# Scores of a key tile's two query halves in neighbouring PSUM banks, read by one exponential of 1024 columns

## The reference

```python
q = ln @ Wq
kv_input = jnp.concatenate((xn, ln), axis=1)
kv = kv_input @ Wkv
k, v = jnp.split(kv, 2, axis=-1)
...
q, k, v = (heads(q) * scale, heads(k), heads(v))
sim = jnp.einsum('bhid,bhjd->bhij', q, k)
mask_full = jnp.concatenate((mask, jnp.ones((b, m), dtype=bool)), axis=1)
...
sim = jnp.where(mask_full[:, None, None, :], sim, max_neg)
attn = jax.nn.softmax(sim.astype(jnp.float32), axis=-1).astype(sim.dtype)
out = jnp.einsum('bhij,bhjd->bhid', attn, v)
```

## Time and profile before

| | |
|---|---|
| time, 3 runs | median 810.05 us (809.28 to 811.12) |
| the profiled execution | 812.56 us, its span 810.8 us |
| granted TensorE clock, mean | 0.978 of full speed |
| PE busy | 751.5 us (93% of the span), 7122 matmuls |
| ACT busy | 609.7 us (75%), 1086 instructions |
| POOL busy | 545.3 us (67%), 745 |
| DVE busy | 559.9 us (69%), 1399 |
| HBM | 34 GB/s over the span |

### The profile page before, as it was taken

How to read it: one execution, slowest core, us unless ns; L and a number is a source line. 1 busy time by engine, 2 the same in 40 slices (tenths; PEclk the granted TensorE clock), 3 DMA queues, 4 the chain that set the end, 5 groups by cost and what they waited for, 6 DMA issues and landing times.

```text
span 810.8 us, 22755 instructions
## 1 busy us (share of the span) xinstructions
PE 751.5 (93%) x7122; PEld 418.6 (52%) x7122; DVE 559.9 (69%) x1399; ACT 609.7 (75%) x1086; POOL 545.3 (67%) x745
## 2 busy tenths in 40 slices
PE   5598999999999999999999999999999999899766
PEld 3344544556464555545554655555555546455423
DVE  5776776666666767666666667676766666586677
ACT  5479788887868687888878696868788887865262
POOL 4366676686867768686868677686868686766122
PEclk9799999999999999999999999999999999999797
DMA  5303322121222202121212212121212121110001
GB/s 178 79 6 93 78 75 73 43 61 56 57 60 56 58 17 63 45 71 42 63 52 58 58 55 62 32 58 32 71 45 72 40 60 56 47 43 19 4 1 53
DMA packets 95820, 44.42 MB, mean 55 GB/s; under 512 B 66500, under 2 KB 87848, under 8 KB 95656
## 3 DMA queue, kind: packets, MB, share of 16 engines
q1 hardware_dynamic: 95728, 43.93, 19.5%
q10 hardware_dynamic: 56, 0.05, 0.0%
HBM read 24.20 MB, written 3.34 MB: 34 GB/s over the span
## 4 chain that ended last, share of the span: by engine, by line
PE 65%; DVE 14%; issue 10%; ACT 5%; POOL 3%; DMA 1%; DVEq 1%; ACTq 0%; SPq 0%; POOLq 0%
PE bank L1496 14%; PE bank L1576 7%; PE bank L1459 6%; PE bank L1463 5%; PE bank L1461 5%; PE bank L1414 4%; PE bank L1593 3%; DVE mx L1940 3%; PE bank L1431 3%; PE bank L1611 2%; PE bank L1390 2%; DVE qkl_l L1936 2%; PE bank L1430 2%; PE bank L1648 1%; ACT qkl_h L1118 1%
## 5 line engine op out<-in xcount | busy, mean ns | idle before, releaser
L867 POOL TENSOR_TENSOR p<-arena,p 128x512 f16<-128x512 f32 x256 | 297.9, 1169 | 133.0 <-ACT arena L1137 131.9
L1146 ACT ACTIVATE p<-bank,maskbias 128x512 f16<-128x512 f32 x224 | 155.2, 693 | 103.5 <-PE bank L1463 101.5
L1496 PE MATMUL bank<-p,xv 128*128 128x512 f16 (+1 forms) x768 | 182.3, 380 | 5.3 <-POOL arena L915 3.7
L1940 DVE TENSOR_REDUCE mx<-bank 128x1 f32<-128x464 f32 x256 | 154.0, 632 | 17.8 <-PE bank L1431 16.1
L1137 ACT ACTIVATE arena<-bank,maskbias 128x512 f32<-128x512 f32 x224 | 155.0, 692 | 0.0
L1496 PEld LDWEIGHTS bank<-p,xv 128*128 128x128 f16 (+1 forms) x768 | 58.2, 97 | 74.5 <-issue 25.6
L1936 DVE TENSOR_TENSOR qkl_l<-bank,qkl_h 128x512 f16<-128x512 f32 x64 | 41.1, 686 | 68.9 <-ACT qkl_h L1118 68.8
L1459 PE MATMUL bank<-qkc_h,xtT_h 128*128 128x512 f16 (+1 forms) x256 | 86.5, 389 | 0.0
L1463 PE MATMUL bank<-qkc_h,xtT_l 128*128 128x512 f16 (+1 forms) x256 | 85.0, 379 | 0.0
L1461 PE MATMUL bank<-qkc_l,xtT_h 128*128 128x512 f16 (+1 forms) x256 | 85.0, 379 | 0.0
L1431 PE MATMUL bank<-xtT_h,qkc_h 128*128 128x400 f16 x256 | 83.4, 338 | 0.0
(11 more groups left out here) (283 smaller groups left out, 1576.0 us busy)
## 6 DMA issues: line engine op xcount, KB each, us to landing
arena<-den_dram SPq DMA_DIRECT2D x62, 128.0 KB, 3.2
qkc_h<-arena SPq DMA_DIRECT2D x30, 256.0 KB, 2.4
qkc_l<-arena SPq DMA_DIRECT2D x30, 256.0 KB, 2.5
raw<-in_ctx SPq DMA_DIRECT2D x32, 192.0 KB, 2.4
lt<-lt_dram SPq DMA_DIRECT2D x60, 32.0 KB, 2.1
arena<-in_L_xattn_Wkv SPq DMA_DIRECT2D x1, 1024.0 KB, 7.8
raw<-in_ctx SPq DMA_DIRECT2D x64, 8.0 KB, 2.0
ltT_dram<-x_all SPq DMA_DIRECT2D x4, 256.0 KB, 2.8
```

Source lines behind the costliest of these rows:

```text
L867: g.tensor_tensor(p_halves[0:r, slot, 1, :], p_all[0:r, (plan.halves_made(0, k, t) - 1) % 2, :], p_halves[0:r, slot, 0, :], ALU.subtract). ...
L1146: a.activation(p_halves[0:r, slot, 0, :], sbank[t % SRING][0:r, :], ACT.Exp, bias=bias)
L1496: op = mm(bk[:, :], halves_of[at, row, :], p_halves[at, slot, prob, :], start=tile < 2 and n == 0, stop=last and n == 2)
L1940: v.tensor_reduce(mx[:, hq_tile, part:part + 1], bk[:, 0:width], AX.X, ALU.max).then_inc(s_jobs_taken, 1)
```

## The change

The eight banks are allocated as four pairs. Where a step belongs to a full key tile (`wide`), PE makes the scores of both query halves one right after the other, at the even step; the odd step has no scores. ACT waits for both and applies each exponential once, to 1024 columns in two banks; its counters go up by two. POOL takes one low half over both halves, at the odd step. `values` stay at their steps. The two slots of `p_all`, which took turns, are now filled together. Steps 0 and 1 of a batch stay as they were. Per batch 3 pairs of steps are concerned, 96 in all.

```diff
+    def wide(self, t):
+
+        return self.PAIRED and self.steps[t][1] is not None
...
-        bank = [es.enter_context(nc.psum_tensor(f"bank{k}", [P, 512], F32)) for k in range(8)]
+        bank_pairs = [es.enter_context(nc.psum_tensor(f"banks{k}", [P, 1024], F32)) for k in range(4)]
+        bank = [bank_pairs[k // 2][:, 512 * (k % 2):512 * (k % 2) + 512] for k in range(8)]
+        score_pair = bank_pairs[1]
...
             def low_probs(plan, i, k, t):
 
-                if (k, t) in plan.SPLIT:
+                if plan.wide(t):
+                    if plan.steps[t][1] == 0:
+                        slot = slot_of(plan, k, t)
+                        pool.wait_ge(s_probs_ready, (i * 2 + k) * plan.STEPS + t + 2)
+                        g.tensor_tensor(p_halves[:, slot:slot + 2, 1, :], p_all[:, :, :], p_halves[:, slot:slot + 2, 0, :], ALU.subtract).then_inc(s_p_lo, 2)
+                elif (k, t) in plan.SPLIT:
...
+            def wide_probs(plan, i, k, t, part):
+
+                gg, slot, chunk = (i * 2 + k) * plan.STEPS + t, slot_of(plan, k, t), plan.chunk(plan.steps[t][0])
+                bias = maskbias[:, k, chunk:chunk + 1]
+                if part == 0:
+                    act.wait_ge(s_scores_ready, gg + 2)
+                    if happened(gg - RING + 2):
+                        act.wait_ge(s_values_done, gg - RING + 2)
+                    a.activation(p_halves[:, slot:slot + 2, 0, :], score_pair[:, :].rearrange("p (a b) -> p a b", a=2), ACT.Exp, bias=bias)
+                else:
+                    made = plan.halves_made(i, k, t)
+                    if happened(made - 1):
+                        act.wait_ge(s_p_lo, made - 1)
+                    a.activation(p_all[:, :, :], score_pair[:, :].rearrange("p (a b) -> p a b", a=2), ACT.Exp, bias=bias).then_inc(s_probs_ready, 2)
+
             def probs(plan, i, k, t, part):
+                if plan.wide(t):
+                    if plan.steps[t][1] == 0:
+                        wide_probs(plan, i, k, t, part)
+                    return
...
-                        scores(plan, i, k, t)
+                        for u in (t, t + 1) if plan.wide(t) else (t,):
+                            if not plan.wide(t) or plan.steps[t][1] == 0:
+                                scores(plan, i, k, u)
```

## The result

| | before | after | forecast |
|---|---|---|---|
| time, median | 810.38 us (809.28 to 811.12, 4 runs) | 866.5 us (866.22 to 867.08, 4 runs) | 866 |
| ratio | | 1.0695 (1.0676 to 1.0713) | |
| profiled span, mean clock | 810.8 us, 0.978 | 864.5 us, 0.976 | |
| PE busy | 751.5 us (93%) | 758.3 us (88%) | near 87% |
| ACT busy | 609.7 us, 1086 instr. | 577.7 us, 894 | 44 us less |

The change costs 7%, although ACT has 192 instructions and 32 us of work less. From the page after: span, busy times, the chain that ended last by engine, and two of its groups, the new low half and the new exponential.

What follows compares the result with a forecast made beforehand. PE's queue was taken as the bound. Three places less 0.2 us gave 3.85 us per body, 54 over fourteen, 57.6 with the first and last; 868 against the median, lowered to 866 us, range 838 to 884.

Steps and rivals of the forecast that it cites:

- Place one: s = 14 and 15: `T` waits for `raw`, behind the wide exponentials on ACT; `T` starts 1.60 us later per body.
- Place three: s = 10 to 13: longer low half delays `srs`, then L1969 and the reductions of `MAX`; PE loses 1.4 us per body.
- Place two: s = 2 to 4: PE waits 1.0 us for wide exponentials, 0.45 for the low half; 1.05 net of the `QC` gap.
- Rival (a): Only places one and two cost, since by s = 11 POOL and ACT catch up; 848 us, chance 0.25.
- Rival (b): Wide instructions are dearer: exponential 1.38 us, POOL 2.4; 1.6 us more per body, 880 to 892 us, chance 0.10.
- Rival (c): Other sign: PE's gaps close and ACT's 21 us matter; 804 us, chance 0.04.
- (d): Nothing measurable: the new waits fall where PE waits anyway; time stays at 810 us, chance 0.04.
- The ends: First body, without `tail`, costs 2.65 us; last, without `MAX` of the odd batch and `T`, about 1.
- five of eight: Count of places in a body where other PE work was said to cover the loss of alternating score banks.

Runs made afterwards that it cites:

- `P1` first: Changed kernel with POOL making `sve` and `srs` ahead of the wide low half at s = 11 instead of behind it: 850.37 us, ratio 1.0484.
- the order on PE alone: Kernel before with only the scores of both halves made together on PE; exponentials and low halves stay single: 828.4 us, ratio 1.0223.
- three undone: Changed kernel with steps 2, 3 of the even and 2, 3 and 6, 7 of the odd batch narrow again: 831.37 us, ratio 1.0237.
- the single undoings: Changed kernel, one pair narrow again per run: odd steps 6, 7 847.8 us; odd steps 2, 3 850.02; even steps 2, 3 845.84.

## Why the prediction was right, and where its terms were off

**Direction, size, places.** Forecast 866, measured 866.5. Each of the three places waits after. At places one and three it is for what was named: `T` for `raw` behind the exponentials, `MAX` for `mx` behind `srs`. At place two the low half was named rightly and the first wait was not. Rival (a), without place three, falls by the 1.56 us of DVE for `srs` and by the 0.91 us a body that moving `P1` gave back. Rival (b), dearer instructions, falls by the groups: 1.11 us and 2.13 us, each under my value. Rival (c) needed `T` in time; it was 1.50 us late. (d), nothing measurable, falls by the 56 us.

**Prices.** Wide exponential 1.15 forecast, 1.11 measured; from start to start 1.05 and 1.01. Low half 2.28 forecast, 2.13 measured: it is shorter than two single ones in a row. The estimate of 1.13 us from the Trainium skill (ScalarE: Activation LUTs, What ACT_TABLE_LOAD costs) lies nearer the measured 1.11 than mine.

ACT's busy time fell by 32 us and not by 44, because I took the full 2 x 0.69 for two exponentials whose records overlap: 192 x (2 x 0.58 - 1.01) = 29 comes nearer.

**Place one** (1.60, measured 1.50) was right in mechanism and size; the difference is mostly the 0.08 of two starts. The run with `raw` between the exponentials shows its cause.

**Place three** (1.4, measured 0.81) was right in its cause and too large. The step that failed is "of 2.2 us some 1.85 reach the reductions". `srs` was 2.04 later and the reductions 1.21. I had taken off the time by which `srs` was early (0.42 of it is gone). I had not seen that L1969's 0.68 us to the next start held a wait of its own, until the single low half beside it on POOL was done; after, with POOL idle, it is 0.27. Rows 9 and 10 did not show that low half. Where a low half runs beside it again, it takes longer again: 0.91 us with `P1` first, 0.77 with steps 2 and 3 of the odd batch narrow.

**Place two** (1.05, measured 0.90 net) was right in size, in part by luck. The forecast's chain ran through ACT's second exponential to the scores of s = 4. These come 4.69 us after those of s = 2, forecast 4.85, and the exponential ends at 426.77, just before them, but PE does not wait for it. What holds PE, beside the parts of `MAX`, is the copies in the middle of that chain, and they are late mostly by the order on PE (0.65 of 0.89 us). I had also missed that the moved scores took the spacing from between the parts of `MAX`. From the scores of s = 2 to those of s = 4 it is 3.88 us before, 4.53 with the order on PE alone and 4.69 in the changed kernel; from s = 4 to 6 it is 5.54, 5.45 and 5.94. So the order costs 0.56 of the 1.21 us, the wide exponential 0.16, and the wide low half, which the forecast had at 0.45, 0.49.

The page quoted against the change (the Trainium skill, Perfetto Trace Analysis, Matmuls) says that groups should rotate through banks, so that one is read out while the next is made. Place two bears on it: the parts of `MAX` do rotate, but through two banks only, and with no scores between them the third waits 0.54 us for the read-out. At places one and three the same PE order costs nothing.

**The sum** came out right by luck, by two errors against each other. It gave 57.6 us, measured are 56; the 2 us that I took off at the end, for waits that would be gone, were a guess. The body was 0.76 us too dear, 14 x 0.76 = 11 us. The ends were too cheap. ACT's copy of the latents (L1168, L1198 after) stands at one point of each body and marks fifteen periods. Their first point moved from 71.42 to 72.83 (+1.4), their last from 732.41 to 781.15 (+47.3 more), the end of the span by 5.0 more. Of the 47.3, the thirteen inner periods are 13 x 3.09 = 40.2, the first 3.0, the last 2.2, and 2.0 remain: two periods of after were 1.53 longer each, at a lower clock, and one of before was 1.06 longer, at full clock, by a wait of 1.12 for a DMA (`qkc_h`, at 258.92). Counted like the forecast: 14 x 3.09 = 43.3, the ends 8.4 where I had 3.65, these odd periods 2.0. The last body has no `MAX`, `T` or later scores as cover, and PE waits there 0.80 and 2.29 us for the low half and 1.21 for `xh`.

**Places called covered.** The forecast has "five of eight", but a body has six wide pairs, and its own sums leave three of them covered. They were so in the loop of the changed kernel only: it is not a property of the places, as the run with three undone showed. There the three cost 0.87 us a body. Adding up the three places was right for the changed kernel, by the single undoings (3.12 us a body against 3.09), though not place by place: undoing place three also took 0.50 from the wait at place one.

## What to carry to other kernels

Price a wider instruction by when its first consumer gets its data and by what stands behind it in the same queue, not by the engine's busy time: here ACT had 32 us less work and the kernel took 56 us more time. In a tight schedule of in-order queues several waits end within a few tenths of each other, so undoing one cause gives back part of its price, and undoing all can show a wait that was hidden; test each again beside the others. Apply such a change only where PE has other work for the whole round trip: one place of six, in the loop alone, gave 0.4%, all six cost 7%.

## What the runs showed of the hardware that was not expected

- An exponential of 1024 columns that reads over a bank's end takes 1.11 us with float16 as with float32 output (x96 each, mean 1114 ns), against 1.055 us for a copy of 1024 columns in the earlier trace rows. No loss shows at the border of the banks.
- A subtraction of 1024 columns on POOL takes 2.13 us, one of 512 1.16: 0.19 us less than two.
- A small instruction of DVE on data outside PSUM can last until an instruction of POOL beside it is done. The 128x128 `xh` (L1969, L2001, L2005) takes 0.35 us with POOL idle and ends 0.08 us after POOL's low half where the two meet: 0.76 us before, 0.91 with `P1` first. Of those on `raw`, with a median of 0.33 us, the longest took 1.94, POOL's instruction beside it 1.89 (the order on PE alone). The reductions of `MAX`, which read PSUM, keep their 0.6 us beside POOL. No run was made to test this; the traces agree in it.
- The granted clock fell to 0.51 for 7 us behind a wait of PE of 2.00 us, with PE busy ahead of it and after it. In the changed kernel two bodies of sixteen took 48.92 us in place of 47.39 at a mean clock of 0.97; their waits are those of all the others, 1.53 us for `raw` among them:

```profile
403.71:451.10 47.39, 43.71 (x428) 24.28 (x426) 29.67 (x78) 33.79 (x53) 31.57 (x37) 1.00 0.18 50
451.10:500.02 48.92, 45.35 (x428) 25.45 (x426) 29.68 (x78) 34.06 (x54) 31.57 (x37) 0.97 0.17 48
...
463.00:467.00 4.00, 4.00 (x29) 2.44 (x28) 1.78 (x5) 2.68 (x5) 3.75 (x7) 0.64 0.75 229
```

The fall lies right behind `T` (462.29) again. With steps 2 and 3 of the even batch narrow, the same waits of 1.53 us lower it in no body of the loop. Why the clock falls behind such a wait in one body and not in the next, these runs do not tell.
